# Group-whitening kernel on one Trainium2 core: the store transfers move from SyncE's queue to ACT's, one behind each operation

## The chip, the cores and the metric

The kernel runs on one core of one Trainium2 chip. Its compute engines are PE (TensorE, matrix products), DVE (VectorE), ACT (ScalarE) and POOL (GpSimd); SP (SyncE) computes nothing and only issues DMA transfers. Each engine works through its own list of instructions in the order of the program, and semaphores order the engines against each other. The 16 DMA engines of the core move the data between main memory and the on-chip memory. The metric is the device time of one execution in microseconds (us); the kernel before took 418.66 us, the median of 3 runs (415.48 to 418.74).

## What is computed

The input x has 32 samples, 128 channels and 56 x 56 pixels, 51.4 MB in all, and the output is as large. The reference, cut down:

```python
def _gn(v, G=32, eps=1e-05):                 # normalise 4 channels of one sample together
    g = v.reshape(B_, G, C_ // G, H_, W_)
    return ((g - mean(g)) / jnp.sqrt(var(g) + eps)).reshape(v.shape)

def _zca_forward(x, weight, bias, groups=16):   # per group of 8 channels
    xf = jnp.transpose(x, (1, 0, 2, 3)).reshape(C, M)      # M = 32*56*56
    xg = (xf - mean(xf, axis=1)).reshape(G, c, M)
    cov = jnp.einsum('gim,gjm->gij', xg, xg) / M + EPS * eye(c)
    e, v = jnp.linalg.eigh(cov)
    proj = jnp.einsum('gik,gk,gjk->gij', v, rsqrt(e), v)
    return proj @ xg * weight + bias

x = x + _zca_forward(_gn(x), L0_conv_weight, L0_conv_bias)
```

## The kernel before

The 16 channel groups (`GROUPS`) of 8 channels are independent of each other. One group is 32 samples x 8 channels = 256 rows of 3136 pixels; it is held as two **tiles** (`TILES`, index `s`) of 128 rows, 1.57 MB each. `ring` holds `RING` = 7 groups; group g lies in slot g % 7, and it is overwritten in place: loaded, normalised, and replaced by the output. So the loads of group g + 7 may start only when the stores of group g have landed.

A group passes through these stages. DVE takes the row statistics (`row_stats`, L338) and works out scales. POOL and ACT normalise the pieces in place (L314 and L499), ACT casts the high half to fp16 (`high_part`, L511), POOL subtracts it to get the low half (`low_part`, L322), DVE transposes (`turn`, L395), and PE adds up the Gram matrix (`gram`). Then comes a chain of 19 small steps, the **hops**, for the inverse square root: PE multiplies (`hop`), and DVE or ACT copies the result back (`read_hop`, on ACT the copies into `wv`, `zz`, `tz`, `zx` at L530). At last PE applies the matrix in 8 parts per group (`apply`, tile `ps_apply`, two buffers in PSUM), and ACT writes each part back into `ring` (`finish`, L520, which counts up `out_ready`). Parts u = 0 to 3 complete tile 0, and u = 4 to 7 tile 1.

The order is written out by hand: each operation of a group has a tick, group g + 1 has the same one 64 ticks (`TICKS`) later, and each engine runs through the ticks in one loop and emits what is due. So an engine works on several groups at once, and nothing but the tables `..._AT` sets the order on it. Semaphores, not ticks, decide when an instruction really runs.

A tile is loaded by 8 transfers of 196 KB (`load`, L278: 2 halves of the pixels, 4 channel pairs) and stored by 4 transfers of 392 KB (`store`, L285). SP issues both. The first 7 groups are loaded up front; after that SP's list alternates. `store(g, s)` waits for `out_ready` to say that the 4 parts of the tile are done, and `load(g + 7, s)` waits for `out_stored[r][s]`, until all 4 stores of the tile that was in that place have landed:

```python
STORE_AT = [222, 256]
LOAD_AT = [STORE_AT[s] + 24 - RING * TICKS for s in range(TILES)]
```

Of the kernel before, what the change touches and what calls it, by code (L numbers as in the profile page):

```python
# [16 lines left out]
GROUPS = C // CG  # L17
GN = 4
TILES = N * CG // P
# [6 lines left out]
RING = 7  # L26
# [16 lines left out]
PARTS = TILES * HW // (2 * BANK)  # L43


PAIRS = CG // 2
# [26 lines left out]
TICKS = 64  # L73
# [19 lines left out]
HOP_READ_AT = [106, 110, 112, 115, 120, 122, 132, 132, 141, 143, 146, 151, 152, 156, 158, 164, 166, 173, 181]  # L93
APPLY_AT = [191, 197, 203, 210, 220, 228, 236, 243]
FINISH_AT = [196, 207, 208, 220, 223, 236, 240, 254]
STORE_AT = [222, 256]
LOAD_AT = [STORE_AT[s] + 24 - RING * TICKS for s in range(TILES)]
FIRST_TICK, LAST_TICK = -64, TICKS * (GROUPS - 1) + 258

COLS = {}  # L100
_at = 0
# [34 lines left out]
def zca_residual(nc: bass.Bass, x: bass.AP, weight: bass.AP, bias: bass.AP, const: bass.AP, out: bass.AP):  # L136
    with ExitStack() as ctx:
        def sb(name, shape, dt=F32):
            return ctx.enter_context(nc.sbuf_tensor(name, shape, dt))
# [4 lines left out]
        def sem(name):  # L144
            return ctx.enter_context(nc.semaphore(name))

        ring = sb("ring", [P, RING, TILES, HW])
# [39 lines left out]
        out_stored = [[sem(f"out_stored_{r}_{s}") for s in range(TILES)] for r in range(RING)]  # L187
# [22 lines left out]
        out_ready = sem("out_ready")  # L210

        x_dram = x.rearrange("(s n) (g c) h w -> g s n c (h w)", s=TILES, c=CG)
        out_dram = out.rearrange("(s n) (g c) h w -> g s n c (h w)", s=TILES, c=CG)
# [29 lines left out]
        def span(p):  # L243

            s, q = divmod(p, len(PIECE_UNITS))
            lo, hi = PIECE_UNITS[q]
            return s, slice(lo * UNIT, hi * UNIT)

        def width(p):
            lo, hi = PIECE_UNITS[p % len(PIECE_UNITS)]  # L250
            return (hi - lo) * UNIT
# [5 lines left out]
        def due(places, t):  # L257

            items = places.items() if isinstance(places, dict) else enumerate(places)
            return [((t - a) // TICKS, k) for k, a in items  # L260
                    if (t - a) % TICKS == 0 and 0 <= (t - a) // TICKS < GROUPS]

        def due_one(place, t):
            return [g for g, _ in due([place], t)]
# [4 lines left out]
        @block.sync  # L269
        def _(sp):  # L270
            def load(g, s):
                r = g % RING
                if g >= RING:
                    sp.wait_ge(out_stored[r][s], 16 * PAIRS * (g // RING))
                for q in range(HALVES):
                    px = slice(q * HALF, (q + 1) * HALF)
                    for a in range(PAIRS):
                        sp.dma_start(ring[a::PAIRS, r, s, px], x_dram[g, s][:, a::PAIRS, px]).then_inc(  # L278
                            x_landed[r][s][q], 16)

            def store(g, s):
                r = g % RING
                sp.wait_ge(out_ready, PARTS * g + PARTS // TILES * (s + 1))
                for a in range(PAIRS):
                    sp.dma_start(out_dram[g, s][:, a::PAIRS, :], ring[a::PAIRS, r, s, :]).then_inc(  # L285
                        out_stored[r][s], 16)

            for s in range(TILES):
                load(0, s)
            sp.dma_start(cst[:], const).then_inc(const_landed, 16)  # L290
            with nc.allow_non_contiguous_dma(reason="256 channel scalars, once"):
                sp.dma_start(wb8[:, 0, :], weight.rearrange("(g j) o -> j (g o)", j=CG)).then_inc(const_landed, 16)
                sp.dma_start(wb8[:, 1, :], bias.rearrange("(g j) o -> j (g o)", j=CG)).then_inc(const_landed, 16)
            for g in range(1, RING):
                for s in range(TILES):
                    load(g, s)
            for t in ticks:
                for g, s in due(LOAD_AT, t):
                    if g >= RING:
                        load(g, s)  # L300
                for g, s in due(STORE_AT, t):
                    store(g, s)
            for r in range(RING):
                for s in range(TILES):
                    sp.wait_ge(out_stored[r][s], 16 * PAIRS * len(range(r, GROUPS, RING)))
# [182 lines left out]
        @block.scalar  # L488
        def _(act):
            def stats_root(g):  # L490
                act.wait_ge(stat_step, STAT_OPS * g + VAREPS)
                nc.scalar.activation(root[:], vareps, ACT.Sqrt).then_inc(root_done, 1)  # L492

            def normalise(g, p):
                s, px = span(p)
                act.wait_ge(stat_step, STAT_OPS * g + Y_SET)
                y = ring[:, g % RING, s, px]
                i = g % STAT_RING
                nc.scalar.activation(y, y, ACT.Identity, bias=y_add[:, i, s:s + 1],  # L499
                                     scale=y_mul[:, i, s:s + 1]).then_inc(y_act_ready, 1)  # L500

            def high_part(g, p):
                s, px = span(p)
                i = PIECES * g + p
                if p in Y_POOL:
                    act.wait_ge(y_pool_ready, len(Y_POOL) * g + sorted(Y_POOL).index(p) + 1)
                else:
                    act.wait_ge(y_act_ready, len(Y_ACT) * g + sorted(Y_ACT).index(p) + 1)
                if i >= HL_RING:
                    act.wait_ge(t_ready, i - HL_RING + 1)  # L510
                nc.scalar.copy(hl_ring[:, i % HL_RING, 0:width(p), 1], ring[:, g % RING, s, px]).then_inc(h_ready, 1)  # L511

            def finish(g, u):
                s, q = divmod(u, PARTS // TILES)
                if u == 0:
                    act.wait_ge(stat_step, STAT_OPS * (g + 1))
                i = PARTS * g + u
                act.wait_ge(applied, i + 1)
                px = slice(2 * BANK * q, 2 * BANK * (q + 1))
                nc.scalar.activation(ring[:, g % RING, s, px].rearrange("p (a b) -> p a b", a=2),  # L520
                                     ps_apply[:, i % 2 * 2:i % 2 * 2 + 2, 0:BANK],
                                     ACT.Identity, bias=fin_add[:, g % STAT_RING, s:s + 1],
                                     scale=scale[:, g % STAT_RING, s:s + 1]).then_inc(out_ready, 1)

            def read_hop(g, k):
                e = g % 2

                def copy(dst, src):
                    act.wait_ge(solve_mm[e], HOPS * (g // 2) + k + 1)
                    nc.scalar.copy(dst, src).then_inc(solve_read[e], 1)  # L530

                if k in HOP_WV[:-1]:
                    copy(wv[:, e], s_wv[e])
                if k == HOP_WV[-1]:
                    copy(zz[:, e], s_z[e])
                if k == HOP_T:
                    copy(tz[:, e], s_t[e])
                if k == HOP_V:
                    act.wait_ge(res_copied, g + 1)
                    copy(zx[:, e], s_zx[e])  # L540

            for t in ticks:
                for g, k in due(HOP_READ_AT, t):
                    read_hop(g, k)
                for g in due_one(ROOT_AT, t):
                    stats_root(g)
                for g, u in due(FINISH_AT, t):
                    finish(g, u)
                for g, p in due(Y_ACT, t):
                    normalise(g, p)  # L550
                for g, p in due(H_AT, t):
                    high_part(g, p)

        @block.tensor
        def _(pe):
# [119 lines left out]
```

## Time and profile before

| | |
|---|---|
| median of 3 runs | 418.66 us (415.48, 418.66, 418.74) |
| the profiled execution, its own time | 416.91 us |
| its span in the trace | 415.1 us |
| PE busy | 348.4 us, 84% |
| DVE / ACT busy | 314.5 us, 76% / 314.8 us, 76% |
| POOL busy | 287.7 us, 69% |
| DMA | 103.72 MB, mean 250 GB/s |
| median issue-to-landing, load / store | 3.7 us / 5.0 us |

The span is the stretch of time the trace covers; the time of an execution has 1.8 us around it. "SPq" is SP's queue; an issue on it is shown with the time that the queue's owner spends on issuing, which is apart from the time to landing. "Waits" name what ended an engine's idle time. "PEclk" is the clock granted to PE, as a share of 2.4 GHz. Names such as `ps_small` are the kernel's tensors, with buffer numbers left out.

### The profile page before, as it was taken

How to read it: one execution, taken by the hardware profiler on the slowest of the kernel's cores; microseconds unless marked ns; L12 is line 12 of the kernel's file. 1: busy time of each engine (PE TensorE's matmuls, PEld its weight loads, DVE VectorE, ACT ScalarE, POOL GpSimd, SP SyncE). 2: the span in 40 equal slices, each digit the busy share in tenths (PEclk: the TensorE clock that was granted, in tenths of full speed). 3: DMA queues.
4: the chain of work that ended last, by engine and by line, in shares of the span. 5: the costliest groups of instructions: out<-in, count | busy, mean ns of one | idle time of the engine just before them, and what ended most of it. 6: DMA issues, size and time to landing. Idle time of an engine off the chain costs nothing.

```text
span 415.1 us, 8571 instructions
## 1 busy us (share of the span) xinstructions
PE 348.4 (84%) x3202; PEld 218.7 (53%) x3202; DVE 314.5 (76%) x869; ACT 314.8 (76%) x449; POOL 287.7 (69%) x148
## 2 busy tenths in 40 slices
PE   0115266999999999999999999989997999999991
PEld 0114255666666666666666666646663666554450
DVE  2679999899999999999999999975895885531000
ACT  1065466789898989898989898967796798954572
POOL 0069979788888888888888888876586697930000
PEclk9999999999999999999999999985898999999997
DMA  7999999536678667876779677877678699984667
GB/s 220 265 301 302 304 317 326 176 107 203 216 254 288 214 217 240 288 225 217 243 250 295 189 239 234 288 220 234 218 264 278 205 347 344 323 285 167 213 209 271
DMA packets 18890, 103.72 MB, mean 250 GB/s; under 512 B 6432, under 2 KB 6432, under 8 KB 14752
## 3 DMA queue, kind: packets, MB, share of 16 engines
q1 hardware_dynamic: 18848, 103.18, 76.7%
q8 instruction: 25, 0.41, 0.4%
q14 instruction: 17, 0.14, 0.1%
HBM read 51.77 MB, written 51.38 MB: 248 GB/s over the span
## 4 chain that ended last, share of the span: by engine, by line
PE 67%; SPq 9%; DVE 8%; DMA 8%; POOL 3%; issue 2%; ACT 1%; DVEq 0%
PE ps_apply L557 41%; PE ps_small L557 12%; PE ps_gram L557 10%; SPq L278 6%; DMA out_dram<-ring 5%; PE ps_stat L557 3%; DVE bn L338 3%; POOL hl_ring L322 3%; DVE t_ring L395 2%; SPq L285 2%; DMA wb<-in_L_conv_bias_dram 1%; DMA ring<-in_x_dram 1%; DVE spread_in L405 1%; POOL ring L314 1%; ACT tz L530 1%
## 5 line engine op out<-in xcount | busy, mean ns | idle before, releaser
L322 POOL TENSOR_TENSOR hl_ring<-ring,hl_ring 128x1024 f16<-128x1024 f32 (+1 forms) x96 | 230.8, 2414 | 53.5 <-ACT hl_ring L511 53.5
L557 PE MATMUL ps_apply<-ring,a_t 128*128 128x392 f32 x512 | 208.8, 534 | 0.0
L520 ACT ACTIVATE ring<-ps_apply,fin_add,scale 128x784 f32<-128x784 f32 x128 | 127.4, 996 | 18.1 <-PE ps_apply L557 17.9
L338 DVE BATCH_NORM_STATS2 bn<-ring 128x6 f32<-128x448 f32 x224 | 129.1, 603 | 15.7 <-DMA ring<-in_x_dram 15.7
L511 ACT CAST hl_ring<-ring 128x1024 f16<-128x1024 f32 (+1 forms) x96 | 128.9, 1368 | 5.9 <-POOL ring L314 2.9
L395 DVE STREAM_TRANSPOSE t_ring<-hl_ring 128x1024 f32<-128x1024 f32 (+1 forms) x96 | 119.2, 1242 | 2.9 <-POOL hl_ring L322 2.8
L557 PEld LDWEIGHTS ps_apply<-ring,a_t 128*128 128x128 f32 x512 | 89.6, 195 | 44.9 <-issue 3.9
L557 PE MATMUL ps_gram<-t_ring 128*128 128x64 f16 x1568 | 69.4, 201 | 10.8 <-DVE t_ring L395 10.8
L314 POOL TENSOR_SCALAR ring<-ring,y_mul,y_add 128x1024 f32<-128x1024 f32 (+1 forms) x48 | 57.9, 1213 | 25.5 <-DVE y_add L382 25.5
L557 PEld LDWEIGHTS ps_gram<-t_ring 128*128 128x128 f16 x1568 | 59.1, 103 | 14.0 <-DVE t_ring L395 11.3
L499 ACT ACTIVATE ring<-ring,y_add,y_mul 128x1024 f32<-128x1024 f32 (+1 forms) x48 | 59.9, 1249 | 7.9 <-DVE y_add L382 7.9
L424 DVE SCALAR_TENSOR_TENSOR pp<-ps_small,cst 16x16 f32<-16x16 f32 x112 | 17.2, 154 | 44.8 <-PE ps_small L557 43.7
L530 ACT COPY wv<-ps_small 16x32 f32<-16x32 f32 x112 | 18.4, 164 | 26.8 <-PE ps_small L557 26.5
L557 PEld LDWEIGHTS ps_small<-wv 16*16 16x16 f32 x224 | 12.1, 91 | 48.2 <-issue 36.8
L557 PE MATMUL ps_small<-pp,wv 16*16 16x16 f32 (+1 forms) x224 | 23.5, 178 | 7.6 <-DVE pp L424 7.6
L557 PE MATMUL ps_small<-wv 16*16 16x16 f32 x224 | 23.8, 180 | 2.3 <-ACT wv L530 2.3
L557 PEld LDWEIGHTS ps_small<-pp,wv 16*16 16x16 f32 (+1 forms) x224 | 11.8, 89 | 14.2 <-DVE pp L424 9.1
L557 PE MATMUL ps_small<-wv,pp 16*16 16x16 f32 x192 | 18.9, 172 | 0.0
L492 ACT ACTIVATE root<-ps_stat 128x2 f32<-128x2 f32 x16 | 2.4, 151 | 19.9 <-DVE ps_stat L360 19.9
L557 PE MATMUL ps_small<-wb,cst 8*128 8x32 f32 x2 | 0.6, 405 | 17.5 <-DMA wb<-in_L_conv_bias_dram 17.5
L557 PEld LDWEIGHTS ps_stat<-dr,cst 128*128 128x128 f32 x64 | 10.6, 216 | 8.8 <-DVE dr L377 5.2
L557 PE MATMUL ps_stat<-dr,cst 128*128 128x1 f32 x64 | 9.6, 253 | 4.8 <-DVE dr L377 4.8
(59 smaller groups left out, 201.7 us busy)
## 6 DMA issues: line engine op xcount, KB each, us to landing
ring<-in_x_dram SPq DMA_DIRECT2D x256, 196.0 KB, 3.7
out_dram<-ring SPq DMA_DIRECT2D x128, 392.0 KB, 5.0
cst<-const_dram SPq DMA_DIRECT2D x1, 380.0 KB
wb<-in_L_conv_weight_dram SPq DMA_DIRECT2D x1, 0.5 KB
wb<-in_L_conv_bias_dram SPq DMA_DIRECT2D x1, 0.5 KB
```

What stands on the lines that cost most here:

```text
L278: sp.dma_start(ring[a::PAIRS, r, s, px], x_dram[g, s][:, a::PAIRS, px]).then_inc(x_landed[r][s][q], 16)
L285: sp.dma_start(out_dram[g, s][:, a::PAIRS, :], ring[a::PAIRS, r, s, :]).then_inc(out_stored[r][s], 16)
L314: nc.gpsimd.tensor_scalar(y, y, y_mul[:, i, s:s + 1], y_add[:, i, s:s + 1], ALU.mult, ALU.add).then_inc(y_pool_ready, 1)
L322: nc.gpsimd.tensor_tensor(hl[:, :, 0], ring[:, g % RING, s, px], hl[:, :, 1], ALU.subtract).then_inc(l_ready, 1)
L338: nc.vector.bn_stats(bn[:, g % 2, s, c, :], ring[:, g % RING, s, c * BN:(c + 1) * BN]).then_inc(bn_done, 1)
L395: nc.vector.transpose(words(t_ring[:, i % T_RING, 0:n]), words(hl_ring[:, i % HL_RING, 0:n])).then_inc(t_ready, 1)
L424: nc.vector.scalar_tensor_tensor(out=pp[:, e], in0=s_m[e], scalar=POLY[it][1], in1=ai[:, CW * it:CW * (it + 1)], op0=ALU.mult, op1=ALU.add ...
L499: nc.scalar.activation(y, y, ACT.Identity, bias=y_add[:, i, s:s + 1], scale=y_mul[:, i, s:s + 1]).then_inc(y_act_ready, 1)
L511: nc.scalar.copy(hl_ring[:, i % HL_RING, 0:width(p), 1], ring[:, g % RING, s, px]).then_inc(h_ready, 1)
L520: nc.scalar.activation(ring[:, g % RING, s, px].rearrange("p (a b) -> p a b", a=2), ps_apply[:, i % 2 * 2:i % 2 * 2 + 2, 0:BANK], ACT.Iden ...
L530: nc.scalar.copy(dst, src).then_inc(solve_read[e], 1)
L557: return nc.tensor.matmul(out_, lhsT, rhs, start=start, stop=stop, skip_group_check=True)
```

## The change

The stores leave SP's list and enter ACT's. The list of ticks now has eight entries, one for each store transfer (four for tile 0, four for tile 1), so that a single transfer stands behind one operation of ACT. SP's list holds loads only. The wait before a store is the same one, on `out_ready`, but now it is ACT that waits for its own `finish`. Transfers of a load still wait for `out_stored`. The data moved, the size of the transfers and the number of them are as before.

```diff
-STORE_AT = [222, 256]
-LOAD_AT = [STORE_AT[s] + 24 - RING * TICKS for s in range(TILES)]
-FIRST_TICK, LAST_TICK = -64, TICKS * (GROUPS - 1) + 258
+STORE_AT = [223, 229, 235, 236, 256, 260, 268, 271]
+LOAD_AT = [STORE_AT[PAIRS * s + PAIRS - 1] + 20 - RING * TICKS for s in range(TILES)]
+FIRST_TICK, LAST_TICK = -64, TICKS * (GROUPS - 1) + 272
@@ block.sync
-            def store(g, s):
-                r = g % RING
-                sp.wait_ge(out_ready, PARTS * g + PARTS // TILES * (s + 1))
-                for a in range(PAIRS):
-                    sp.dma_start(out_dram[g, s][:, a::PAIRS, :], ring[a::PAIRS, r, s, :]).then_inc(
-                        out_stored[r][s], 16)
...
-                for g, s in due(STORE_AT, t):
-                    store(g, s)
@@ block.scalar
+            def store(g, k):
+                s, a = divmod(k, PAIRS)
+                r = g % RING
+                act.wait_ge(out_ready, PARTS * g + PARTS // TILES * (s + 1))
+                act.dma_start(out_dram[g, s][:, a::PAIRS, :], ring[a::PAIRS, r, s, :]).then_inc(
+                    out_stored[r][s], 16)
+
             for t in ticks:
...
                 for g, p in due(H_AT, t):
                     high_part(g, p)
+                for g, k in due(STORE_AT, t):
+                    store(g, k)
```

**SP, from the first store on** (before with a minus, kept rows without a sign; `ring<-in_x_dram` is a load, `out_dram<-ring` a store, x3 means three more of the same):

```order
-L285 DMA out_dram<-ring 16x2x3136 [waits out_ready]
-L285 DMA out_dram<-ring 16x2x3136 x3
 L278 DMA ring<-in_x_dram 32x1x1568 [waits out_stored_0_0]
 L278 DMA ring<-in_x_dram 32x1x1568 x7
-L285 DMA out_dram<-ring 16x2x3136 [waits out_ready]
-L285 DMA out_dram<-ring 16x2x3136 x3
 L278 DMA ring<-in_x_dram 32x1x1568 [waits out_stored_0_1]
 L278 DMA ring<-in_x_dram 32x1x1568 x7
```

The pattern goes on for all tiles. Before, the wait of a load for landed stores held up the stores of the next tile, and the wait of a store for `out_ready` held up the next loads; now SP's only waits are those of loads.

**ACT, where tile 0 of a group is completed**, before (the first row is `finish` of parts 3 and 4):

```order
L520 ACTIVATE ring<-ps_apply,fin_add,scale 128x784 x2
L530 COPY zz<-ps_small 8x8
L511 CAST hl_ring<-ring 128x1024
L530 COPY tz<-ps_small 8x8
L511 CAST hl_ring<-ring 128x1024
L520 ACTIVATE ring<-ps_apply,fin_add,scale 128x784
L530 COPY zx<-ps_small 8x128
```

and of the change at the same place (L511, L521, L502 and L537 are there `finish`, the copies of `read_hop`, the casts and the stores):

```order
L511 ACTIVATE ring<-ps_apply,fin_add,scale 128x784 x2
L537 DMA out_dram<-ring 16x2x3136
L521 COPY zz<-ps_small 8x8
L502 CAST hl_ring<-ring 128x1024
L537 DMA out_dram<-ring 16x2x3136
L521 COPY tz<-ps_small 8x8
L502 CAST hl_ring<-ring 128x1024
L537 DMA out_dram<-ring 16x2x3136
L511 ACTIVATE ring<-ps_apply,fin_add,scale 128x784
L537 DMA out_dram<-ring 16x2x3136
L521 COPY zx<-ps_small 8x128
```

Stores k = 0 to 3 now stand behind `finish` of part 4, two casts and `finish` of part 5. Store 0 waits for part 3, which stands two operations ahead of it.

**ACT, where tile 1 is completed**, after the change (the row ahead of these is `finish` of part 7, the first row a normalisation for a later group, L490):

```order
L490 ACTIVATE ring<-ring,y_add,y_mul 128x1024
L537 DMA out_dram<-ring 16x2x3136
L521 COPY wv<-ps_small 16x32
L511 ACTIVATE ring<-ps_apply,fin_add,scale 128x784
L537 DMA out_dram<-ring 16x2x3136
L483 ACTIVATE root<-ps_stat 128x2
L502 CAST hl_ring<-ring 128x1024
L537 DMA out_dram<-ring 16x2x3136
L521 COPY wv<-ps_small 16x32
L511 ACTIVATE ring<-ps_apply,fin_add,scale 128x784
L537 DMA out_dram<-ring 16x2x3136
L511 ACTIVATE ring<-ps_apply,fin_add,scale 128x784
```

The four transfers k = 4 to 7 are what is new; the compute rows and their order are those of before, here and everywhere else on ACT.

## Rows read from the trace of the kernel before

**Rows 1.** The page's chain of work that ended last, shares of the span

```profile
PE 67%; SPq 9%; DVE 8%; DMA 8%; POOL 3%; issue 2%; ACT 1%; DVEq 0%
```

**Rows 2.** Windows: stretch, length, busy PE, PEld, DVE, ACT, POOL, PEclk, DMA share, GB/s

```profile
92.06:257.21 165.15, 163.19 (x1600) 102.43 (x1600) 154.06 (x433) 154.12 (x225) 144.03 (x73) 1.00 0.74 241
257.21:332.62 75.41, 70.02 (x601) 42.66 (x601) 57.85 (x163) 58.98 (x85) 53.94 (x28) 0.86 0.74 240
278.50:295.00 16.50, 16.26 (x93) 9.12 (x91) 9.35 (x26) 9.81 (x14) 10.67 (x5) 0.51 0.80 262
332.62:353.35 20.73, 20.48 (x200) 12.78 (x201) 15.05 (x47) 19.32 (x29) 17.95 (x10) 1.00 0.96 346
12.00:75.00 63.00, 27.25 (x324) 22.88 (x325) 56.85 (x139) 32.00 (x39) 46.32 (x24) 1.00 1.01 303
```

**Rows 3.** The chain in order of time: start, us, what

```profile
92.06 0.95 PE ps_small L557 x14
...
257.21 0.95 PE ps_small L557 x14
...
332.62 1.06 PE ps_small L557 x14
```

**Rows 4.** Waits of SP's own queue: us in total, times, longest

```profile
SPq L278 <- DMA out_dram<-ring: 78.4, 18, 5.3
SPq L285 <- ACT ring L520: 40.7, 11, 13.6
```

**Rows 5.** Timeline of SP's queue: start, us, what

```profile
97.00 5.03 SPq L278 DMA_DIRECT2D ring<-in_x_dram  x8
102.08 4.06 SPq L285 DMA_DIRECT2D out_dram<-ring  x4
...
323.88 5.03 SPq L278 DMA_DIRECT2D ring<-in_x_dram  x8
```

**Rows 6.** Waits of the engines in the stretch from 257 to 332 us

```profile
DVE bn L338 <- DMA ring<-in_x_dram: 6.9, 4, 3.1
```

**Rows 7.** Timeline of PE in that stretch; in brackets the idle time ahead

```profile
277.08 0.20 PE L557 MATMUL ps_small<-pp,wv 16*8 16x8 f32 x2 [1.45 <-DVE pp L424]
...
318.41 0.21 PE L557 MATMUL ps_small<-pp,wv 16*16 16x16 f32 x2 [2.95 <-DVE pp L424]
```

**Rows 8.** The lines of the loads and the stores: issue time on SP's queue, landing

```profile
L278 SPq DMA_DIRECT2D ring<-in_x_dram x256: 533/592/1626, 0.7 to 328.3; - x128
...
L285 SPq DMA_DIRECT2D out_dram<-ring x128: 534/932/2111, 88.8 to 409.6; - x128
...
DMA to landing us min/median/max: 3.3/5.0/7.0
```

**Rows 9.** Timeline of SP's queue, first and last of the first four stores

```profile
88.77 0.59 SPq L285 DMA_DIRECT2D out_dram<-ring  x1
...
90.87 1.13 SPq L285 DMA_DIRECT2D out_dram<-ring  x1
```

**Rows 10.** Timeline of ACT in a steady group, where tile 1 is completed

```profile
160.86 0.99 ACT L520 ACTIVATE ring<-ps_apply,fin_add,scale 128x784 f32<-128x784 f32 x1
161.76 1.23 ACT L499 ACTIVATE ring<-ring,y_add,y_mul 128x1024 f32<-128x1024 f32 x1
...
166.54 1.01 ACT L520 ACTIVATE ring<-ps_apply,fin_add,scale 128x784 f32<-128x784 f32 x1 [0.37 <-PE ps_apply L557]
```

**Rows 11.** Timeline of ACT in the same group, where tile 0 is completed

```profile
170.32 0.99 ACT L520 ACTIVATE ring<-ps_apply,fin_add,scale 128x784 f32<-128x784 f32 x1
171.76 1.00 ACT L520 ACTIVATE ring<-ps_apply,fin_add,scale 128x784 f32<-128x784 f32 x1 [0.44 <-PE ps_apply L557]
...
174.43 0.15 ACT L530 COPY tz<-ps_small 8x8 f32<-8x8 f32 x1 [0.39 <-PE ps_small L557]
...
176.61 0.24 ACT L530 COPY zx<-ps_small 8x128 f32<-8x128 f32 x1
```

**Rows 12.** Timeline of ACT: its last operation

```profile
406.53 1.00 ACT L520 ACTIVATE ring<-ps_apply,fin_add,scale 128x784 f32<-128x784 f32 x1 [0.31 <-PE ps_apply L557]
```

## The prediction

> **What bounds the kernel now.** I read the chain of work that ended last first. PE holds 67% of it, but SP's queue and the DMAs hold 17% [rows 1], so there is a place where PE is not what ends last. The chain in order of time finds it. The 14 small products of a hop mark the same place in each group: they come at 92.06 and at 257.21, eight groups later, which is 165.15 / 8 = 20.64 us a group; the next three groups, to 332.62, take 75.41 us [rows 3]. The table of windows says what the stretches are. In the eight even groups PE is busy 163.19 of 165.15 us at the full clock: PE is the bound there, and ACT, busy 154.12 / 8 = 19.27 us a group, has 1.4 us of idle time in each. In the next 75.41 us PE is busy 70.02 at a mean clock of 0.86 [rows 2]. Three groups at the even pace take 61.9 us, so **13.5 us are lost there**.
>
> The cause is on SP. SP issues the 8 loads of a tile (5.03 us), then the 4 stores of the next one (4.06 us), then waits until these have landed before it can load again [rows 5]. The waits of its own queue show that last step, 78.4 us in 18 waits [rows 4]. From the first tile reloaded, at 97.00, to the eighteenth, at 323.88, there are 17 steps: 13.35 us a tile, **26.7 us a group, against the 20.64 that PE needs** [rows 5]. The 7 groups in `ring` cover this for a while. Each group the loads fall 6 us further back, until DVE's row statistics wait for them (6.9 us in 4 waits) [rows 6], and behind DVE PE waits 1.45 us at 277 and 2.95 us at 318 [rows 7]. What follows the first of these waits costs more than the wait itself: from 278.5 to 295 PE's granted clock is 0.51, the 1.2 GHz level, and PE is busy for 16.26 us with what would take half of that, some 8.2 us more [rows 2].
>
> **The change, part by part.**
>
> SP's list. It loses 4 issues and one wait on `out_ready` for each tile. What is left is the wait for landed stores and 8 issues of 0.592 us [rows 8], about 5.0 us for each 10.3 us. A load chain now starts when its own stores have landed and never stands behind other stores. A tick is 20.64 / 64 = 0.32 us. The first store starts at 88.77 [rows 9], its tile's last one some 13 ticks, 4.2 us, later; 5.0 us to landing [rows 8] gives a first load at about 98 and the second tile's at about 109, as before (97.00, and 13.35 later). But the eighteenth comes at 109 + 8 x 20.64 = 274 instead of 324 [rows 5]. At 275, where PE starves, SP has issued (275 - 97) / 13.35 = 13.3 tiles where PE's pace is 178 / 10.32 = 17.2, 40 us behind: so much the ring covers. Now the loads keep PE's pace. Worth: **-13.5 us**, if the clock stays up when PE doesn't wait, as it does in the even stretch [rows 2].
>
> The DMA engines. Both directions at PE's pace are 2 x 51.4 MB / 16 = 6.4 MB in 20.64 us, 311 GB/s, where 241 were moved. The nearest rows are 303 GB/s, loads alone at the start, and 346 GB/s, mostly stores, from 332.62 on, and in that window the group still takes 20.73 us, so full DMA traffic doesn't slow the engines [rows 2]. If 303 were the ceiling, a group's data would take 21.2 us; nine groups of loads would slip 5 us, against the 40 that the ring covers. Cost: 0.
>
> ACT's list. It gains 8 issues a group. Three prices matter.
> (a) How long is one issue on ACT? No row shows it. On SP the first of four on an idle queue takes 0.59 us and the fourth in a row 1.13 [rows 9], the median of all is 0.932, behind 8 loads in the same queue [rows 8]. On ACT they stand at least one operation apart and have a queue without loads; I take 0.7, with bounds of 0.53 (the smallest) and 0.932 + 0.592 = 1.52, a store that is held up through one whole issue of a load by SP.
> (b) Does ACT compute while it issues? No row of this trace shows a transfer issued by ACT. What the rows do show is that one operation starts before the one ahead has ended (161.76 against 160.86 + 0.99) [rows 10]: the next one is already waiting at the engine. I take it that operations handed over go on running while the transfer is issued, and that only those behind it are handed over later.
> The Trainium skill says so ("Advanced Engine Details and Errata", Sequencer Loop: engine instructions are pushed into a queue, and further ones wait there while a control instruction runs); no run here shows it yet.
> (c) Then each issue has a cover and a deadline. Where tile 1 is completed: store 4 may start when part 7 is written, 161.85; the four issues have until the `finish` at 166.54, which now waits 0.37 us for PE anyway: 4.7 us, 1.17 each [rows 10]. Where tile 0 is completed: store 0 may start at 171.31; `tz`, due at 174.43, stands behind two issues (3.1 us), and `zx`, due at 176.61, behind four (5.3 us, 1.3 each) [rows 11]. With 0.7 the sums are 2.8 us at either place. What covers them are casts and normalisations of 1.2 to 1.4 us and `finish` of 1.0. Cost: 0. If an issue takes 1.5, the four end 1.3 and 0.7 us late, with 0.04 us between issues [rows 5, 8] some 2.3 together; the 1.4 us of idle time takes up a part, and 1 us a group is left. `finish` is late then, PE waits for a free buffer, and the hop behind `zx` waits too.
>
> The end. The last 8 `finish` run at PE's pace with only 0.31 us of idle time between them [rows 12], and with no casts there three stores of tile 0 stand between parts 4 and 5: 2.1 us of issues beside one `finish` of 1.0. Part 5 comes 0.5 to 1 us late and passes some of that on through the two buffers. The last four stores are issued back to back as before. Cost: **+0.5 us** (0 to 1.2).
>
> **The sum**, against the profiled execution's own time: 416.91 - 13.5 + 0.5 = 403.9 us. The median of the runs is 1.75 us above that execution, and the runs lie 3.3 us apart; the stall and the clock are what can vary, and they go. I say 404.5.
>
> One rule speaks against the change. The Trainium skill ("DMA: Bandwidth & Descriptors", Issuing engines are not separate DMA queues) says that a second issuing engine saves only issue time, "usually small relative to the DMA itself"; by it the gain would be near zero. The rows have DMA at 241 GB/s in the even stretch [rows 2] and SP's queue 26.7 us a group long [rows 5], so here the issuing queue with its waits is what is short, not bandwidth.
>
> **The rivals.**
> - **An issue stops ACT (slower).** Then each group's ACT time is 19.27 plus 8 issues: 24.0 us at 0.59 and 26.7 at 0.932 [rows 2, 8, 9], and ACT is the bound from 89 to about 353 us, 12 groups: +40 to +73 us, less the gain: 444 to 477 us. It is slower than before from 1.1 us a group on. For it: ACT has so little idle time. Against it: operations overlap already [rows 10]. Chance 0.12.
> - **The issues overlap but are long**, since ACT's stores and SP's loads fall together (loads start a landing time after the stores, and that is when the other tile's stores are due). From 1.2 us each on, ACT runs late; at 1.52, 12 groups x 1 us: 404 to 417, middle 410. Chance 0.14, a quarter of it within 1% of before. The Trainium skill ("Perfetto Trace Analysis", DMA Instruction — HWDGE) has a lock on the descriptor generator, which two sequencers share; no row here shows two.
> - **The half clock isn't due to PE's wait** and comes all the same: only 13.5 - 8.2 = 5.3 us are gained, 412 us. Both dips stand right behind a wait of PE [rows 2, 7]. Chance 0.04.
> - **The loads stay late**, being bound by the DMA engines: no change, 417 to 419. For a stall they must slip 40 us in nine groups, 4.4 us a group, a rate of 256 GB/s; 303 and 346 were reached [rows 2]. Chance 0.04.
> - The forecast itself, 402 to 407: 0.66.
>
> **How the numbers follow.** Runs of this kernel lie 0.8% apart, so about 1% is what can be told from no change. Faster by over 1% (under 414.5): 0.66 + 0.09 + 0.03 = 0.78. Within 1%: 0.07. Slower: 0.15, the first rival and a part of the second. The range is 401.5 (the fastest run of before, less 13.5, and 0.5 for the unknown end) to 416, which takes in most of the overlapping case and the clock; it leaves out the stopped ACT and the unchanged case. The forecast's own range is 402 to 407.
>
> **What would show it.** The hop marks 20.6 us apart with no stretch of 75 us; the eighteenth tile of loads issued near 274, not 324; no wait of `bn` for loads after the start; the clock at full from 90 to the end; store issues on ACT's queue of 0.6 to 0.9 us that lie beside its operations, and ACT's sum of operations as before. If ACT's operations stand apart by the length of an issue, the forecast is wrong at step (b); if PE waits for `ps_apply` buffers or `zx`, at (a) or (c); if `bn` still waits for loads, in the DMA term.

## The result and the profile of the changed kernel

| | before | changed |
|---|---|---|
| median | 418.7 us (4 runs, 415.48 to 425.04) | 404.67 us (4 runs, 403.31 to 406.29) |
| ratio to before | | 0.9691, 95% interval 0.9621 to 0.9761 |
| profiled execution, its span | 416.91 us, 415.1 us | 403.31 us, 401.5 us |

The change makes the kernel 3% faster. Some executions of a kernel are some per cent longer than the rest, as the 425.04 here: the ranges of times hold them, the ratios and their intervals leave them out. The page of the changed kernel, its busy times, its DMA queues and its chain of work:

```profile
PE 339.6 (85%) x3202; PEld 214.3 (53%) x3202; DVE 314.5 (78%) x869; ACT 313.6 (78%) x449; POOL 288.0 (72%) x148
...
q10 hardware_dynamic: 6144, 51.39, 40.5%
q1 hardware_dynamic: 12704, 51.79, 39.0%
...
PE 77%; DVE 8%; POOL 4%; ACT 3%; SPq 3%; issue 2%; DMA 1%; ACTq 0%; DVEq 0%
```

q10 is the new queue, with the stores; q1 keeps the loads. The queues and the DMAs were 17% of the chain [rows 1] and are 4% now. ACT's busy time is 313.6 us where it was 314.8: the 128 issues have added nothing to its operations.

The hop marks of the changed kernel, from its chain in order of time:

```profile
90.25 0.95 PE ps_small L557 x14
...
338.28 0.95 PE ps_small L557 x14
...
358.33 0.95 PE ps_small L557 x14
```

and two windows of it, the first over nine groups (stretch, length, busy PE, PEld, DVE, ACT, POOL, PEclk, DMA share, GB/s):

```profile
90.25:276.32 186.07, 183.70 (x1801) 115.20 (x1801) 173.42 (x487) 173.35 (x253) 162.08 (x82) 1.00 0.91 303
...
358.33:401.50 43.17, 31.59 (x138) 15.97 (x138) 3.09 (x17) 20.09 (x30) 0.00 (x0) 0.96 0.65 211
```

From 90.25 to 338.28 there are 12 groups in 248.03 us, 20.67 us each, at the full clock. Before, the same 12 groups, from 92.06 to 353.35, took 261.29 us [rows 2, 3]: **13.3 us less, all of it in the stretch of 75 us**, where three groups now take 62.0 us (276.32 to 338.28). The rest of the difference between the two profiled executions is 1.8 us less ahead of the first mark and 1.5 us more behind the last (43.17 us from 358.33, where the kernel before took 41.70 from 373.40). The first of these isn't the change's: in a second profile of the changed kernel (the run after_again below) the first mark stands at 93.26.

The changed kernel's queues: SP's own waits, the last 16 loads, and the issue and landing times of stores (L537) and loads (L278):

```profile
SPq L278 <- DMA out_dram<-ring: 44.0, 17, 20.0
...
263.08 19.77 SPq L278 DMA_DIRECT2D ring<-in_x_dram  x16
```

```profile
L537 ACTq DMA_DIRECT2D out_dram<-ring x128: 542/546/2120, 87.4 to 396.0; - x128
...
DMA to landing us min/median/max: 3.3/5.0/7.5
```

```profile
L278 SPq DMA_DIRECT2D ring<-in_x_dram x144: 533/1018/2255, 95.3 to 282.2; - x144
```

(the last one for the stretch from 90 to 285 us alone). The last loads are issued by 283 us; before, the last tile's started at 323.88 [rows 5]. An issue on ACT takes 0.546 us in the median and 0.71 in the mean (the 128 durations of the trace add up to 90.8 us). A load's issue on SP takes 1.02 us in this stretch in the median, where that of before was 0.592 [rows 8].

ACT where tile 0 is completed, in a steady group of the changed kernel:

```profile
168.81 1.00 ACT L511 ACTIVATE ring<-ps_apply,fin_add,scale 128x784 f32<-128x784 f32 x1
170.24 1.01 ACT L511 ACTIVATE ring<-ps_apply,fin_add,scale 128x784 f32<-128x784 f32 x1 [0.44 <-PE ps_apply L557]
170.25 0.54 ACTq L537 DMA_DIRECT2D out_dram<-ring  x1
171.15 0.14 ACT L521 COPY zz<-ps_small 8x8 f32<-8x8 f32 x1
171.18 0.54 ACTq L537 DMA_DIRECT2D out_dram<-ring  x1
171.19 1.33 ACT L502 CAST hl_ring<-ring 128x1024 f16<-128x1024 f32 x1
172.91 0.15 ACT L521 COPY tz<-ps_small 8x8 f32<-8x8 f32 x1 [0.40 <-PE ps_small L557]
```

An issue of 0.54 us and an operation of 1.0 or 1.3 us run side by side, and the waits in brackets, 0.44 and 0.40 us, are as long as before (0.44 and 0.39) [rows 11]. One thing here was not foreseen: store 0 could have started at 169.81, when part 3 was written, and starts at 170.25, together with the `finish` ahead of it, which had waited for PE. The experiments come back to this.

### The profile page after: what moved, and what is told of

Read it like the earlier page. It is cut to its first block, busy times and chain, and to the rows that moved or that the text cites. A ratio compares the mean times of both kernels' runs of the same rounds, so it can differ in the third digit from the quotient of the medians.

```text
span 401.5 us, 8571 instructions
## 1 busy us (share of the span) xinstructions
PE 339.6 (85%) x3202; PEld 214.3 (53%) x3202; DVE 314.5 (78%) x869; ACT 313.6 (78%) x449; POOL 288.0 (72%) x148
## 4 chain that ended last, share of the span: by engine, by line
PE 77%; DVE 8%; POOL 4%; ACT 3%; SPq 3%; issue 2%; DMA 1%; ACTq 0%; DVEq 0%
PE ps_apply L557 47%; PE ps_small L557 15%; PE ps_gram L557 12%; PE ps_stat L557 3%; POOL hl_ring L313 3%; DVE bn L329 3%; DVE t_ring L386 3%; SPq L278 2%; ACT ring L511 1%; DMA wb<-in_L_conv_bias_dram 1%; DVE spread_in L396 1%; ACT tz L521 1%; POOL ring L305 1%; DVE pp L415 0%; ACTq L537 0%
## 5 line engine op out<-in xcount | busy, mean ns | idle before, releaser
L557 PE MATMUL ps_apply<-ring,a_t 128*128 128x392 f32 x512 | 202.4, 520 | 0.6 <-ACT ring L511 0.5
L511 ACT ACTIVATE ring<-ps_apply,fin_add,scale 128x784 f32<-128x784 f32 x128 | 127.4, 995 | 19.3 <-PE ps_apply L557 17.7
L502 ACT CAST hl_ring<-ring 128x1024 f16<-128x1024 f32 (+1 forms) x96 | 129.1, 1370 | 6.0 <-POOL ring L305 2.9
L557 PEld LDWEIGHTS ps_apply<-ring,a_t 128*128 128x128 f32 x512 | 87.3, 190 | 44.4 <-ACT ring L511 3.8
L557 PE MATMUL ps_gram<-t_ring 128*128 128x64 f16 x1568 | 68.5, 200 | 10.8 <-DVE t_ring L386 10.8
L490 ACT ACTIVATE ring<-ring,y_add,y_mul 128x1024 f32<-128x1024 f32 (+1 forms) x48 | 60.0, 1249 | 7.9 <-DVE y_add L373 7.9
L557 PEld LDWEIGHTS ps_gram<-t_ring 128*128 128x128 f16 x1568 | 58.2, 102 | 14.0 <-DVE t_ring L386 11.3
L521 ACT COPY wv<-ps_small 16x32 f32<-16x32 f32 x112 | 18.3, 163 | 17.1 <-PE ps_small L557 17.0
```

The lines of the kernel that those rows point to most:

```text
L557: return nc.tensor.matmul(out_, lhsT, rhs, start=start, stop=stop, skip_group_check=True)
```

## The experiments

The profile shows what happened, not whether the stores had to leave SP, nor how much room ACT has. Both were tested; all ratios are to the kernel before on the same chip.

**1. Was it the queue, or only its order?** The kernel before, with all transfers on SP, one number changed:

```diff
-LOAD_AT = [STORE_AT[s] + 24 - RING * TICKS for s in range(TILES)]
+LOAD_AT = [STORE_AT[s] + 36 - RING * TICKS for s in range(TILES)]
```

> The kernel before, all transfers still on SP, with one number changed: a load comes 36 ticks behind the store of its place instead of 24, so that it stands behind the stores of the next tile (stores tile 0, stores tile 1, loads tile 0, stores, loads tile 1, ...) and the stores it waits for were issued about 10 us earlier. My theory: what made the loads late was the 4 us wait for landing in the middle of one queue, not where the stores are issued. A tile then costs SP 5.0 + 4.1 = 9.1 us of issuing against 10.3 us of PE time, the loads keep up, the stretch of 75 us becomes 62 us: 404 us (402 to 407), and no half clock. The rival, that the issuing itself must leave SP's queue: SP still falls behind, 412 to 419 us.

Measured: 403.18 us (402.04 to 404.60), ratio 0.9653 (0.9619 to 0.9688). SP's own waits in this run, and a piece of its timeline:

```profile
SPq L285 <- ACT ring L520: 91.1, 16, 14.5
...
101.07 3.19 SPq L285 DMA_DIRECT2D out_dram<-ring  x4
...
163.91 3.72 SPq L285 DMA_DIRECT2D out_dram<-ring  x4
167.67 6.75 SPq L278 DMA_DIRECT2D ring<-in_x_dram  x8
174.46 3.63 SPq L285 DMA_DIRECT2D out_dram<-ring  x4
...
278.60 3.32 SPq L285 DMA_DIRECT2D out_dram<-ring  x4
```

The 78.4 us that loads waited for landed stores [rows 4] are gone, stores and loads stand back to back, and a tile takes 10.4 us: 17 of them from 101.07 to 278.60, 177.53 us. That is PE's pace of 10.3 and not the 9.1 us of issuing that I had reckoned with. The issues have become longer (eight loads 6.75 us here, 5.03 before), so SP has next to nothing to spare in this version, and the ring covers the little that it falls behind. The steady part shows no stall: the hop marks at 93.15 and 340.93 in this run's chain are 12 groups apart, 20.65 us each. So the loss was the wait for landing in the middle of one queue. That the stores left the queue was one way to remove it, and not the only one.

**2. Where do the 1.5 us at the end come from?** The changed kernel with the last group's 8 stores on SP:

```diff
+            g = GROUPS - 1
+            for s in range(TILES):
+                sp.wait_ge(out_ready, PARTS * g + PARTS // TILES * (s + 1))
+                for a in range(PAIRS):
+                    sp.dma_start(out_dram[g, s][:, a::PAIRS, :], ring[a::PAIRS, g % RING, s, :])...
...
                 for g, k in due(STORE_AT, t):
-                    store(g, k)
+                    if g < GROUPS - 1:
+                        store(g, k)
```

> The changed kernel, with the 8 stores of the last group back on SP, which has nothing else to issue by then. The changed kernel's end is 1.5 us longer than that of before (from the hop mark 43.2 us against 41.7); my theory is that the issues of the last group delay ACT's finish operations, since no casts cover them there, and PE waits for buffers. Expected: 1.0 to 1.5 us less than the changed kernel, 403.4 us. If the longer end comes from the landing of the stores and not from their issue on ACT: no difference, 404.7 us.

> The changed kernel itself, on the chip of the two others, so that about 1 us between them can be told. 404.7 us by both theories.

Measured, on one chip: 405.32 us (403.34 to 406.26) against 406.55 us (406.13 to 410.39). The end stretch of the one, of after_again and of the run with one number changed, each from its last hop mark to its end:

```profile
362.43:404.30 41.87, 31.37 (x138) 15.97 (x138) 3.10 (x17) 20.12 (x30) 0.00 (x0) 0.96 0.67 217
```

```profile
361.62:404.80 43.18, 31.59 (x138) 15.98 (x138) 3.09 (x17) 20.11 (x30) 0.00 (x0) 0.95 0.65 211
```

```profile
360.98:402.80 41.82, 31.06 (x138) 15.93 (x138) 3.09 (x17) 20.08 (x30) 0.00 (x0) 0.94 0.64 216
```

With the issues of the last group off ACT the stretch is 41.9 us, as with all on SP, and 1.3 us shorter than the changed kernel's. So the longer end comes from the issues on ACT. In the changed kernel's own timeline of ACT three issues in a row put 1.06 us of waiting ahead of the `finish` of part 5, which before had waited 0.31, as the last one did [rows 12]:

```profile
387.83 2.02 ACTq L537 DMA_DIRECT2D out_dram<-ring  x3
389.89 1.00 ACT L511 ACTIVATE ring<-ps_apply,fin_add,scale 128x784 f32<-128x784 f32 x1 [1.06 <-PE ps_apply L557]
```

The releaser in brackets is the nearest semaphore; the operation begins 0.04 us behind the end of the issues, and it is they that held it.

That is about half of it. From the hop mark to the start of the last `finish` it takes 33.13 us before (373.40 to 406.53 [rows 12]), 34.24 in the changed kernel (358.33 to 392.57) and 33.53 with the last group's stores on SP (362.43 to 395.96). So 0.7 us come from the stores of the last group, and 0.4 from those of the group before it, which stand among `finish` operations too. The rest of the 1.5 us lies behind the last `finish` (8.57 us before, 8.93 in the changed kernel, 8.34 with these stores on SP); no run tells what makes it.

**3. Does the placement behind single operations matter?**

```diff
-STORE_AT = [223, 229, 235, 236, 256, 260, 268, 271]
-LOAD_AT = [STORE_AT[PAIRS * s + PAIRS - 1] + 20 - RING * TICKS for s in range(TILES)]
+STORE_AT = [223] * 4 + [256] * 4
+LOAD_AT = [a + 20 - RING * TICKS for a in (236, 271)]
```

> The changed kernel with the 4 stores of a tile issued by ACT back to back (all four at tick 223 and at tick 256) instead of one behind each operation; loads on SP stay where they are. Theory: the issues run beside operations already handed over, so a burst has only one operation in its cover. Four issues take 2.2 us (4 x 0.546) to 3.2 us (as on SP's idle queue), of which 1.0 to 1.3 are covered, so ACT's next operation comes 1 to 2 us late twice a group, of which about 1.4 us goes into idle time: +0.6 to +2.5 us a group, 12 groups, 411 to 434 us. Rival: the placement behind single operations doesn't matter, since ACT's queue is deep enough or PE hides it: 404 to 406 us.

Measured: **503.21 us** (497.46 to 514.22), ratio 1.2017 (1.1917 to 1.2117). The same eight issues, placed otherwise, make the kernel 20% slower than before. ACT's timeline at the two bursts of a group:

```profile
159.43 1.23 ACT L490 ACTIVATE ring<-ring,y_add,y_mul 128x1024 f32<-128x1024 f32 x1
159.55 3.23 ACTq L537 DMA_DIRECT2D out_dram<-ring  x4
162.82 0.17 ACT L521 COPY wv<-ps_small 16x32 f32<-16x32 f32 x1 [2.17 <-issue]
...
171.28 3.93 ACTq L537 DMA_DIRECT2D out_dram<-ring  x4
175.26 0.15 ACT L521 COPY zz<-ps_small 8x8 f32<-8x8 f32 x1 [3.12 <-issue]
```

ACT stands still for 2.17 and 3.12 us, 5.3 us a group, since one operation is all that covers four issues. My sign was right and my size was not: I had at most 3.9 us of it, from issues of 3.2 us together, and took 1.4 us off for ACT's idle time. In this execution, at 514.22 us the longest of the four, the groups take 27.7 us (ten of them between the hop marks at 121.04 and 398.49), 7 more than 20.67. ACT's copies stand inside the hop chain, so PE waits for them, and PE's granted clock over two of these groups, from 150.48 and from 176.74 on, is 0.94 and 0.88. So a part of the 7 us is the clock.

**4. More issues of the same bytes.** The store of the changed kernel cut in two, and in four:

```diff
+SPLIT = 2        # 4 in the other run
...
-                act.dma_start(out_dram[g, s][:, a::PAIRS, :], ring[a::PAIRS, r, s, :]).then_inc(
-                    out_stored[r][s], 16)
+                for c in range(SPLIT):
+                    px = slice(c * HW // SPLIT, (c + 1) * HW // SPLIT)
+                    act.dma_start(out_dram[g, s][:, a::PAIRS, px], ring[a::PAIRS, r, s, px]).then_inc(
+                        out_stored[r][s], 16)
```

> The changed kernel with each store transfer cut in two (half the pixels each), the second right behind the first: 16 issues a group on ACT instead of 8, the same bytes. Overlap theory: a pair takes 1.1 us, the deadlines worked out before were 1.17 and 1.3 us a store, so little shows: 404 to 409 us. Rival, that an issue costs ACT its own length after all and the 8 of the change happened to fit into idle time: 16 x 0.55 = 8.8 us more on 19.3 us of operations, 28 us a group instead of 20.6, about 490 us.

> As the run with halves, with each store cut in four: 32 issues a group on ACT. Overlap theory with deadlines: 4 x 0.55 = 2.2 us a store, 8.8 us for each place against 4.7 and 5.3 us of cover, so 7.6 us late a group less 1.4 us of idle time, some 6 us a group: 470 to 485 us. If issues and operations simply added up: 19.3 + 17.6 = 37 us a group, 600 us. If issues cost ACT nothing at all, whatever their number: 405 us.

Measured: 452.97 us (449.26 to 455.14), ratio 1.0849 (1.0774 to 1.0925), and 629.13 us (two runs, 624.16 and 634.11). Both expectations of mine fell: halves were to cost at most 4 us and cost 48, quarters were to give 470 to 485 and gave 629. The rival, that issues and operations add up, was too high for halves (490 us) and nearest for quarters (600 us). Yet they don't simply add up there either: at 161.24 in that run a `finish` of 1.00 us runs beside four issues of 3.09. ACT's timeline of the run with halves, where tile 0 is completed:

```profile
167.69 1.00 ACT L512 ACTIVATE ring<-ps_apply,fin_add,scale 128x784 f32<-128x784 f32 x1 [0.34 <-PE ps_apply L560]
167.69 1.19 ACTq L540 DMA_DIRECT2D out_dram<-ring  x2
168.92 0.15 ACT L522 COPY zz<-ps_small 8x8 f32<-8x8 f32 x1 [0.23 <-ACT ring L512]
...
170.44 1.70 ACTq L540 DMA_DIRECT2D out_dram<-ring  x2
172.20 1.00 ACT L512 ACTIVATE ring<-ps_apply,fin_add,scale 128x784 f32<-128x784 f32 x1 [0.42 <-issue]
172.22 1.39 ACTq L540 DMA_DIRECT2D out_dram<-ring  x2
173.70 0.25 ACT L522 COPY zx<-ps_small 8x128 f32<-8x128 f32 x1 [0.50 <-ACT ring L512]
```

Three of four pairs are longer than the operation beside them, and each time the excess is idle time of ACT: 1.19 us beside a `finish`, 0.23 idle; 1.70 beside a cast, 0.42; 1.39 beside a `finish`, 0.50. The pair beside the second cast, 1.20 against 1.33 us, leaves something over, and nothing of it is saved for the next. The pairs begin when the operation ahead of them begins, as store 0 did in the changed kernel. So a new theory: **an issue does not start while the operation ahead of it still waits for another engine; from there on one operation is its cover, and covers can't be pooled across such a wait.**

This isn't the whole of the 48 us, as two windows of the same run show, between copies into `zx` seven groups and two groups apart (columns as above):

```profile
120.32:296.51 176.19, 156.09 (x1400) 95.43 (x1400) 136.19 (x378) 139.94 (x197) 126.16 (x64) 0.92 0.74 258
321.27:364.27 43.00, 40.95 (x400) 25.51 (x400) 38.77 (x107) 39.75 (x56) 34.97 (x19) 1.00 0.49 158
```

While SP issues loads (the last starts at 317.2), a pair takes 1.50 us in the mean of 56, and a group 25.17 us: PE stands idle 2.9 us of it, and is busy 22.3 us at a granted clock of 0.92, where seven groups of the changed kernel have 20.4 at the full clock. Behind the last load a pair takes 1.17 us, and a group 21.5 us, 0.85 more than 20.65. Most of the 48 us came where the pairs were long, and a good part of that is PE's clock.

**5. That theory, put to the test.** First the same 16 half-size issues, each behind an operation of its own:

```diff
-STORE_AT = [223, 229, 235, 236, 256, 260, 268, 271]
+STORE_AT = [223, 229, 235, 236, 238, 240, 243, 245, 256, 260, 268, 271, 272, 274, 281, 284]
...
-                s, a = divmod(k, PAIRS)
+                s, i = divmod(k, 2 * PAIRS)
+                a, c = divmod(i, 2)
+                px = slice(c * HW // 2, (c + 1) * HW // 2)
```

> The same 16 half-size store issues a group as in the run with halves (453 us), but each behind an operation of its own (finish, cast or normalisation, 0.9 to 1.4 us) instead of in pairs. New theory, from the rows of that run: an issue begins only when the operation ahead of it begins, so it has that one operation as its cover and no more, and what exceeds it is added to ACT's time, each time. A pair of 1.2 us exceeds a finish, a single of 0.55 to 0.9 us doesn't: 404 to 412 us. Old theory, that the covers of a place can be pooled, or that it is the number of issues that counts: as with pairs, 440 to 455 us.

Measured: 407.30 us (406.4 to 407.8), ratio 0.9799 (0.9759 to 0.9838). **The number of issues is the same as in the run of 453 us; only the places differ.** So it isn't the number that costs. But this run doesn't single out the cover: only four of tile 0's eight halves now stand ahead of `zx`, so that the deadlines of the prediction let it through too, and an issue is shorter, 0.57 us in the mean from 120 to 296 us, where one of a pair took 0.75. Its store issues take 0.543 us in the median, and ACT's idle time with no releaser is down to this and 0.4 us ahead of casts:

```profile
ACT ring L511 <- issue: 0.9, 2, 0.4
```

against, with the halves in pairs,

```profile
ACT ring L512 <- issue: 18.7, 28, 2.8
ACT wv L522 <- issue: 5.8, 12, 1.1
ACT zx L522 <- ACT ring L512: 5.1, 11, 0.8
```

The run that tells the covers apart has whole stores again, but those of tile 0 behind copies of 0.15 us:

```diff
-STORE_AT = [223, 229, 235, 236, 256, 260, 268, 271]
+STORE_AT = [228, 230, 237, 250, 256, 260, 268, 271]
```

> The changed kernel with the four stores of tile 0 moved behind ACT's short copies (zz, tz, zx, wv, of 0.15 to 0.25 us) instead of behind casts and finish; the number of issues, 8 a group, and the total time in which they must be done stay. New theory (one issue, one operation as its cover): each of the four leaves ACT idle for 0.3 to 0.4 us, 1.4 us a group, most of which ACT's own idle time of 1.4 us takes up, but two of them stand just ahead of copies that PE waits for: +0.3 to +1.0 us a group, 408 to 418 us, and waits of ACT with nothing to release them (issue) of 0.3 us before the cast behind zz and tz. Pooled cover: no difference, 404 to 407 us.

Measured: 409.10 us (408.36 to 415.70), ratio 0.9832 (0.9791 to 0.9874). ACT's timeline behind the first two:

```profile
173.23 0.54 ACTq L537 DMA_DIRECT2D out_dram<-ring  x1
173.28 0.14 ACT L521 COPY zz<-ps_small 8x8 f32<-8x8 f32 x1
173.87 1.33 ACT L502 CAST hl_ring<-ring 128x1024 f16<-128x1024 f32 x1 [0.45 <-issue]
175.05 0.54 ACTq L537 DMA_DIRECT2D out_dram<-ring  x1
175.07 0.14 ACT L521 COPY tz<-ps_small 8x8 f32<-8x8 f32 x1
175.69 1.36 ACT L502 CAST hl_ring<-ring 128x1024 f16<-128x1024 f32 x1 [0.48 <-issue]
```

The idle times stand where the theory puts them, 0.45 and 0.48 us. The first store's own condition was met at 172.13, when part 3 was written; it starts at 173.23, when PE's product for `zz` is there, and the operations of the time between can't cover it. Three copies into `zx`, at 177.80, 198.88 and 219.96, are 21.08 us apart, 0.43 more than in the changed kernel, where pooled covers allow no difference. The price in time is small, 409.1 us against 407.3 of the run before it on the same chip and 404.7 and 406.6 of the changed kernel on two others: the other two stores of tile 0 stand behind `zx` and `wv`, which don't wait, and one of them (161.05, with its copy at 161.61) is issued ahead of the copy's start, beside the cast before it. Where nobody waits, the hand-over does run ahead of ACT by an operation or two. The first half of the theory has the changed kernel's own trace behind it as well: in all 16 groups the condition of store 0 is met 0.3 to 0.5 us before it starts, the `finish` ahead of it waits for PE, and the issue starts less than 0.01 us behind that `finish`.

**6. What does one starved load cost PE, and its clock?**

```diff
                     sp.wait_ge(out_stored[r][s], 16 * PAIRS * (g // RING))
+                if (g, s) == (10, 0):
+                    sp.wait_ge(out_ready, PARTS * 6)
```

> The changed kernel with one extra wait on SP: the first tile of group 10 may be loaded only when group 5 is wholly written, about 15 us later than it is now and some 6 us too late for the row statistics. All other loads are as before. Theory of the clock: PE waits 4 to 6 us once, and the granted clock then falls to the 1.2 GHz level for some 17 us, as behind the wait at 277 us in the kernel before: 4 to 6 us of waiting plus some 8 us, 416 to 420 us, with PEclk near 0.5 in the windows behind the wait. Rival, that the half clock had another cause: 409 to 411 us and PEclk 1.0.

Measured: 416.73 us (414.97 to 417.64), ratio 0.9985 (0.9962 to 1.0008). The total lies in my range, but not by my working. DVE's row statistics waited 8.5 us, not 6:

```profile
DVE bn L331 <- DMA ring<-in_x_dram: 8.5, 1, 8.5
```

```profile
213.11 0.23 PE L559 MATMUL ps_small<-pp,wv 16*16 16x16 f32 x2 [8.31 <-DVE pp L417]
```

```profile
210.00:217.00 7.00, 3.89 (x26) 2.08 (x26) 4.61 (x11) 2.36 (x4) 1.14 (x1) 0.53 0.92 281
```

PE waited 8.31 us, its clock was near the 1.2 GHz level in the 7 us around the end of the wait, and back at 2.4 GHz in the next 7; two copies of ACT into `zx`, at 198.41 and 228.93, are 30.52 us apart where a group takes 20.65, so that group is 9.9 us longer, 1.6 more than the wait. In the kernel before the half clock lasted 16.5 us behind a wait of 1.45 us [rows 2, 7]. A wait of PE does bring the clock down, which the rival denied; how long it stays down differed by more than a factor of two, and the longer stay followed the shorter wait.

## Why the prediction was right, and which step was not

The forecast was 404.5 us, the measured median is 404.67. The profiled execution was forecast at 403.9 and took 403.31.

**The loss of 13.5 us and its place.** Right: the 12 groups are 13.3 us shorter, all in the starved stretch. The cause was right in kind, since the wait for landed stores is what one number on SP alone removes (experiment 1). The prediction valued it only as a thing that leaves with the stores. The other half of what stands ahead of it, stores whose wait for `out_ready` holds up loads, hardly occurred: 1.9 us in 3 waits from 95 to 329 us of the kernel before.

**The loads.** Right in effect: the last 16 are issued from 263.08 to 282.85, where I had the eighteenth tile begin at 274 and end at 279. The term of 0.592 us for an issue was too small; it is 1.02 us beside ACT's stores in the median and 1.09 in the mean. Eight take 8.1 to 8.8 us of the 10.3 us of a tile, not 4.7, so SP has less room than the working says. SP's waits in front of loads fell from 78.4 to 44.0 us [rows 4], and 20.0 of these stand ahead of the first reload, most of them before any store was issued (87.4).

**The DMA engines.** Right: 303 GB/s from 90 to 276 us at a share of 0.91, against 241 GB/s and 0.74 [rows 2], and a group takes 20.67 us.

**The rule against the change.** The Trainium skill's sentence (in "DMA: Bandwidth & Descriptors", Issuing engines are not separate DMA queues) holds here better than I gave it credit for: what moved the time was a wait in a queue. Experiment 1 shows that no second issuing engine was needed.

**(a) The issue on ACT.** 0.7 us was forecast; the mean is 0.71, the median 0.546 and the longest 2.12. One row was misread on the way: the 0.932 of [rows 8] is the median of all stores, and the 69 that stand behind loads, from 95 to 330 us, have 0.786. **(b) ACT computes while it issues.** Right, as the timeline above shows. For operations handed over ahead of the issue the Trainium skill's "Advanced Engine Details and Errata", Sequencer Loop, agrees. That others are read and queued while it runs, as that section also has it, these runs don't bear out: behind a burst the copy begins at 162.82, 0.04 us after the last issue has ended. The rival in which an issue stops ACT is refuted for issues behind operations.

**(c) Covers and deadlines. This step was wrong, and its error cost nothing only because the change needs little of it.** I put four issues against the 4.7 and 5.3 us between first start and deadline, as if they could use all of it. What the runs put in its place: an issue waits until the operation ahead has what it waits for, and then that operation covers it. With single stores behind copies (c) allows no loss, and the group is 0.43 us longer (experiment 5). With pairs of 1.17 us, just the 1.17 and 1.3 that (c) lets through, it is 0.85 us longer (experiment 4). And the price for longer issues was too low by far: for 1.5 us (c) has 1 us a group, having taken 1.4 us of idle time off the 2.3 that the issues are late. The halves with pairs of 1.50 us took 4.5 us more a group: 2.6 us more idle time of PE, so that nothing is left of the 1.4 taken off, and 1.9 us of PE's lower clock, which (c) leaves out. So the bound for the second rival, 417 us, was too mild as well. In the change an issue of 0.55 us in most places stands beside 1.0 to 1.4 us, and the sum of this term stays 0.

**The end.** +0.5 us was forecast (0 to 1.2), 1.3 to 1.5 were measured. The mechanism was right (experiment 2): the last group's stores make the `finish` operations 0.7 us later. The size missed 0.4 us from the group before the last, and 0.4 us behind the last `finish`, where I had no change.

**The clock.** That it stays up without the wait is right. The 8.2 us were what it cost in that one execution and no fixed price (experiment 6).

How near the number came was luck in part. The end cost 1.0 us more than forecast, and the profiled execution started its steady part 1.8 us earlier than the one of before, which isn't the change's; the two cancel. after_again starts it 3.0 us later, and on its chip the changed kernel took 406.55 us against 418.40 before, 11.9 us less and not 14.

**A version that beats both** is experiment 1: 403.18 us (ratio 0.9653, up to 0.9688) against 406.55 us of the changed kernel on the same chip (0.9746, from 0.9700), 0.8% less. It has the even groups and keeps the shorter end. Its one queue has no room left, though (experiment 1).

## What to carry to other kernels

Look in a transfer queue for waits on landed data that stand ahead of other transfers: moving the waiting transfer a few places back, behind work that can go out at once, may be worth as much as a second queue, and it loads no compute engine. Check then that the queue still keeps pace: its loads' issues grew by a third here, 0.59 to 0.78 us in the mean. If a compute engine is to issue transfers, put each behind one long operation of its own, since 16 issues a group gave 407 us singly and 453 in pairs, and eight in rows of four 503. Count the covers one by one and don't pool them. And a stretch in which the tensor engine starves costs more than its waits, by an amount that varies.

## What the runs showed of the hardware

- An issue on ACT doesn't start while the operation ahead waits for another engine's result (170.25 beside 170.24, with the store's own condition met at 169.81, and so in all 16 groups); where nobody waits it may start ahead of that operation (161.05 against 161.61).
- A load's issue on SP took 1.02 us in the median while ACT issued stores of 392 KB, and 0.592 us in the run with all transfers on SP (0.78 in the mean), though both moved about 310 GB/s. A lock on the descriptor generator, which the Trainium skill names ("Perfetto Trace Analysis", DMA Instruction — HWDGE), and two queues that share the DMA engines would both look like this. The spread halves of experiment 5 speak against the lock as the cause: ACT spent more time on issuing there (145 us in all against 91), at the same 312 GB/s, and the loads' issues took 0.60 us. What is left as a difference is the size of ACT's transfers; no run shows why that matters.
- ACT's own issues of 392 KB took 0.55 us in the median with loads under way and without; in the mean they took 0.79 us from 100 to 280 us and 0.55 from 321 to 345, when there were none.
- The half clock of PE lasted 16.5 us behind a wait of 1.45 us and about 4 us behind one of 2.95 us in the kernel before (granted clock 0.64 from 318 to 320 us, 0.50 to 322, 1.00 to 326), though PE was busy for 16.26 of the 16.5 us [rows 2]; it lasted about 7 us around a wait of 8.31 us in the run with one late load.
